# Scale and inverse on one engine, a rounding step taken half a step later, and reordered seams in a four-stage transformer kernel

## The reference

```
x = x + landmark_attention(layernorm(x))    # 16 heads, 32 landmarks, pseudo-inverse, convolution
x = x + ffn(layernorm(x))                   # 128 -> 352 -> 128
x = x + linear_attention(layernorm(x))      # 16 heads of 8, causal running sum
x = x + ffn(layernorm(x))                   # the same weights again
```

```
scale = max(max(|xb|, over 16) / 6, 1e-12)
q     = grid[nearest(|xb / scale|)] * sign(xb) * scale
y     = q(silu(q(x) @ q(Wg).T) * (q(x) @ q(Wu).T)) @ q(Wd).T
```

## Time and profile before

| | |
|---|---|
| median of 3 runs | 839.45 us (836.2 to 840.21) |
| the profiled execution | 839.01 us, span 837.2 us |
| PE busy | 620.6 us, 74% |
| DVE busy | 541.6 us, 65% |
| POOL busy | 317.3 us, 38% |
| ACT busy | 296.0 us, 35% |
| mean granted TensorE clock | 0.899 |

### The profile page before, as it was taken

The page is one execution under the profiler, slowest core; times in us unless marked ns, Lnnn a source line. Parts: engine busy times, 40 slices in busy tenths (PEclk is TensorE's granted clock), DMA queues, the critical chain, the costliest instruction groups (busy, mean ns, idle before and its releaser), DMA issues.

```text
span 837.2 us, 14007 instructions
## 1 busy us (share of the span) xinstructions
PE 620.6 (74%) x5231; PEld 445.8 (53%) x5231; DVE 541.6 (65%) x1078; ACT 296.0 (35%) x523; POOL 317.3 (38%) x408
## 2 busy tenths in 40 slices
PE   2367887888667577598777765899889887777775
PEld 1366784666634334496555554455555554445554
DVE  7624653333188679577888965566667665798874
ACT  2131111333323323314555543333333344555432
POOL 6540000000100000035667888345555544456563
PEclk9996998999988879799898997698999997899997
DMA  8400000000000000000000000000000000000000
GB/s 259 106 1 1 1 0 1 0 1 0 1 2 0 1 1 1 0 2 1 1 1 1 1 1 0 1 2 2 2 2 1 2 2 2 0 16 24 13 25 26
DMA packets 13675, 10.47 MB, mean 13 GB/s; under 512 B 1398, under 2 KB 12598, under 8 KB 13492
## 3 DMA queue, kind: packets, MB, share of 16 engines
q1 hardware_dynamic: 13620, 9.73, 4.2%
HBM read 7.63 MB, written 2.10 MB: 12 GB/s over the span
## 4 chain that ended last, share of the span: by engine, by line
PE 44%; DVE 29%; POOL 11%; issue 9%; ACT 5%; DMA 0%; ACTq 0%; DVEq 0%; POOLq 0%
PE ps L1145 6%; PE ps L1231 5%; PE ps L1362 4%; PE ps L1172 3%; PE ps L1299 3%; PE ps L1381 3%; DVE r L822 3%; DVE ps L904 2%; POOL G L281 2%; PE ps L1260 2%; PE ps L1181 2%; POOL ln L335 2%; DVE S L830 2%; DVE arena L1005 2%; PE ps L1189 2%
## 5 line engine op out<-in xcount | busy, mean ns | idle before, releaser
L335 POOL TENSOR_TENSOR ln<-mv,lnc 128x4 f32<-128x4 f32 x64 | 13.1, 205 | 150.9 <-DVE mv L702 150.9
L354 POOL MEMSET early<- 128x2560 f32 x2 | 4.5, 2232 | 173.3 <-PE ps L1216 163.3
L1231 PE MATMUL ps<-G,xw 128*126 128x512 f32 x72 | 47.6, 814 | 30.2 <-ACT xw L520 22.5
L381 POOL TENSOR_SCALAR_AFFINE_SELECT arena<-arena 128x1024 f32<-128x1024 f32 x32 | 35.0, 1092 | 72.7 <-ACT arena L646 72.7
L1280 PE MATMUL ps<-wguT,xnt 128*128 128x352 f32 x128 | 54.5, 510 | 8.9 <-DVE S L923 8.9
L1299 PEld LDWEIGHTS ps<-wdT,xnt 128*128 128x128 f32 (+1 forms) x384 | 54.2, 216 | 12.5 <-ACT xnt L575 6.4
L1299 PE MATMUL ps<-wdT,xnt 128*128 128x128 f32 (+1 forms) x384 | 55.5, 300 | 2.3 <-ACT xnt L575 2.2
L1278 PE MATMUL ps<-wguT,xnt 128*128 128x352 f32 x128 | 54.0, 506 | 0.5 <-ACT xnt L568 0.2
L1005 DVE TENSOR_TENSOR arena<-ps,tri 128x1024 f32<-128x1024 f32 x32 | 39.2, 1224 | 23.3 <-PE ps L1362 23.3
L646 ACT ACTIVATE arena<-ps 128x1024 f32<-128x1024 f32 x32 | 32.8, 1024 | 49.5 <-PE ps L1362 49.5
L281 POOL TENSOR_TENSOR G<-S,hoff 128x704 f32<-128x704 f32 x32 | 48.6, 1517 | 3.6 <-DVE S L923 1.2
(11 more groups left out here) (197 smaller groups left out, 1570.8 us busy)
## 6 DMA issues: line engine op xcount, KB each, us to landing
X<-in_x SPq DMA_DIRECT2D x8, 256.0 KB, 4.6
out<-X SPq DMA_DIRECT2D x8, 256.0 KB, 2.3
wqkv<-in_wqkv SPq DMA_DIRECT2D x1, 1024.0 KB
band<-in_band SPq DMA_DIRECT2D x1, 897.8 KB
early<-in_wfc SPq DMA_DIRECT2D x1, 512.0 KB
kI<-in_scaled_eye SPq DMA_DIRECT2D x1, 192.0 KB
wattn<-in_wattn SPq DMA_DIRECT2D x1, 192.0 KB, 7.3
S<-in_wd SPq DMA_DIRECT2D x1, 176.0 KB, 3.5
```

The source lines that it names most:

```text
L381: nc.gpsimd.affine_select(out=masked[n % 2][:, 8:16, :], in_=raw.rearrange("p (h t) -> p h t", t=P), pattern=[[0, 8], [1, P]], compare_op= ...
L1231: last = mm(ps[0:WI, w, :], xw[:, w * WO:w * WO + WI], G1[:, b, :], start=True, stop=True)
```

## The change

Six edits, in the order in which they appear below.

- The scale of a block (h and x) is computed by DVE, directly ahead of the reciprocal, and no longer by POOL. The largest magnitudes are written to spare PSUM columns behind the pair (for the first two quads of x to the old place) and read from there.
- DVE's clamp and `move_h` of pair r move from the end of step r to step r+1, between its two `gated`.
- PE takes `down_mms` ahead of the first `gate_up` of a step.
- `lin_norm` is done by ACT, with the bias add left on POOL as `lin_bias`. For quads 0 and 1 it moves to ACT's steps 11 and 15.
- At the seam from the first feed-forward block to the linear attention, POOL's `lin_qk(0)` goes ahead of the residual and the moments of step 16, and PE's product for the denominators goes behind the last step.
- At the seam to the second one, the four steps that are called early are called after tiles 28, 29, 30 and 31 in place of 27, 28, 29 and 31, and ACT normalises the first quad after tile 27.

```diff
-LIN_FILL = {27: -4, 28: -3, 29: -2, 31: -1}
+LIN_FILL = {28: -4, 29: -3, 30: -2, 31: -1}
...
@@ POOL
                 def step(r):
                     q = (r + FILL) // 2
-                    if r % 2 == 0 and q < QN:
-                        need(g, "fx_quant", ffn_quads(p, q))
-                        scales("fx", xblk, ffn_quads(p, q + 1))
-                    if 0 <= r < PN:
-                        need(g, "fh_quant", ffn_pairs(p, r - 1))
-                        scales("fh", hblk[r % 2], ffn_pairs(p, r + 1))
                     if 0 <= r - 1 < PN:
                         quantise_h(r - 1)
                     if r % 2 and q < QN:
                         quantise_x(q)
-                    if p == 0 and 0 <= r - 3 < PN:
+
+                def finish(r):
+                    if 0 <= r - 3 < PN:
                         residual(r - 3)
...
                 step0(r)
-                if r == 12:
-                    lin_norm(0)
+                if r == 16:
+                    lin_qk(0)
+                finish0(r)
...
                 if r == 16:
-                    lin_norm(1)
-                    lin_qk(0)
+                    lin_bias(0)
...
@@ ACT
+            def lin_norm(q):
+                a.wait_ge(s["moment_step"], 2 * TILES + (q + 1) * QD)
+                need(a, "lin_xT_done", q)
+                for k in range(QD):
+                    t = q * QD + k
+                    last = act(xb[:, k, :], X[:, t, :], ACT.Identity, scale=rstd[:, t:t + 1], bias=shift[:, t:t + 1])
+                last.then_inc(s["lin_xb_done"], 1)
...
+                if r == 11:
+                    lin_norm(0)
...
                 if r == 15:
                     lin_exps(0)
+                    lin_norm(1)
...
                 lin_yT(n)
+                if q + 1 < TILES // QD and phase == 3:
+                    lin_norm(q + 1)
...
+                if n == 27:
+                    a.wait_ge(s["lin_qn_done"], QN)
+                    normalise1(0)
...
@@ DVE
-                def inverse(name, b, n):
+                def inverse(name, b, largest, n, free):
+                    v.wait_ge(s[name + "_absmax"], n + 1)
+                    need(v, name + "_quant", free)
+                    ts(out=b[:, 2, :], in0=largest, scalar1=1.0 / 6.0, scalar2=1e-12, op0=ALU.mult,
+                       op1=ALU.max).then_inc(s[name + "_scale"], 1)
                     v.wait_ge(s[name + "_scale"], n + 1)
                     recip(out=b[:, 1, :], in_=b[:, 2, :]).then_inc(s[name + "_inverse"], 1)
+
+                def largest_h(r):
+                    return up_banks(r, F, 2 * F // BLK)[:, 0, :]
...
                         gated(2 * r)
+                    if 0 <= r - 1 < PN:
+                        move_h(r - 1)
+                    if 0 <= r < PN:
                         gated(2 * r + 1)
                         absmax_h(r)
...
-                    if 0 <= r < PN:
-                        move_h(r)
                 return step
...
@@ PE
                 def step(r):
                     q = (r + FILL) // 2
+                    if 0 <= r - 2 < PN:
+                        down_mms(r - 2)
                     if 0 <= r + 1 < PN:
                         gate_up(2 * r + 2)
-                    if 0 <= r - 2 < PN:
-                        down_mms(r - 2)
...
-                if r == 16:
+                if r == 17:
                     lin_den_mms(0)
-                if r == 17:
-                    lin_rdenT(0)
+            lin_rdenT(0)
```

More of the change, by code:

```diff
@@ L261, in ffn @@
             def ffn(p):
-                def scales(name, b, n):
-                    g.wait_ge(s[name + "_absmax"], n)
-                    nc.gpsimd.tensor_scalar(out=b[:, 2, :], in0=b[:, 0, :], scalar1=1.0 / 6.0, scalar2=1e-12, op0=ALU.mult,
-                                            op1=ALU.max).then_inc(s[name + "_scale"], 1)
                 def quantise_x(q):
@@ L303, in step @@
                         quantise_x(q)
-                    if p == 0 and 0 <= r - 3 < PN:
+                def finish(r):
+                    if 0 <= r - 3 < PN:
                         residual(r - 3)
-                    if p == 0 and r >= 6 and r % 2 == 0:
+                    if r >= 6 and r % 2 == 0:
                         layernorm_moments(2, (r - 6) // 2)
-                return step
+                return step, finish
             g.memset(wn, 0.0).then_inc(s["wn_zeroed"], 1)
@@ L354, in _, with lin_bias @@
                 g.memset(vbd[k], 0.0).then_inc(s["vbd_zeroed"], 1)
-            step0, step1 = ffn(0), ffn(1)
-            def lin_norm(q):
-                g.wait_ge(s["moment_step"], 2 * TILES + (q + 1) * QD)
-                need(g, "lin_xT_done", q)
-                for k in range(QD):
-                    t = q * QD + k
-                    last = nc.gpsimd.tensor_scalar(out=xb[:, k, :], in0=X[:, t, :], scalar1=rstd[:, t:t + 1],
-                                                   scalar2=shift[:, t:t + 1], op0=ALU.mult, op1=ALU.add)
-                last.then_inc(s["lin_xb_done"], 1)
+            (step0, finish0), (step1, _) = ffn(0), ffn(1)
+            def lin_bias(q):
                 g.wait_ge(s["lin_xb_done"], q + 1)
@@ L414, in _ @@
                     if phase == 3 and q + 1 < TILES // QD:
-                        lin_norm(q + 1)
+                        lin_bias(q + 1)
                 if n % QD == 1 and n > QD:
@@ L653, in _ @@
             a.wait_ge(s["b_loaded"], 16 * 6)
+            normalise0(0)
             for r in ATT_FILL.values():
@@ L876, in absmax_x @@
                     v.wait_ge(s["fx_norm"], n + 1)
-                    reduce(out=xblk[:, 0, :].unsqueeze(1), in_=blocks(x_blocks()), axis=AX, op=ALU.max,
+                    reduce(out=largest_x(q).unsqueeze(1), in_=blocks(x_blocks()), axis=AX, op=ALU.max,
                            apply_absolute_value=True).then_inc(s["fx_absmax"], 1)
@@ L907, in absmax_h @@
                     v.wait_ge(s["f_h"], ffn_tiles(p, 2 * r + 2))
-                    reduce(out=pair(hblk[r % 2][:, 0, :]), in_=blocks(up_banks(r)), axis=AX, op=ALU.max,
+                    reduce(out=pair(largest_h(r)), in_=blocks(up_banks(r)), axis=AX, op=ALU.max,
                            apply_absolute_value=True).then_inc(s["fh_absmax"], 1)
```

22 lines of the change are left out of this document (12 added, 10 removed).

## The result

The changed kernel takes 814.62 us (median of 4, 812.91 to 816.35); the kernel before, timed beside it, 839.83 (836.2 to 841.73). The ratio is 0.9714, 95% interval 0.9683 to 0.9746: 2.9% faster. The profiled execution took 816.01 us for a span of 814.3, where 818.5 was forecast for it.

What follows compares the result with a forecast made beforehand. DVE was taken as fullest in both feed-forward blocks, PE in the linear attention. Terms of -1, -10.5, -1.5, 0, -3 and -4.5 sum to -20.5 from 839.0: 818.5 profiled, 819 us on the median, range 810 to 832.

Steps and rivals of the forecast that it cites:

- the clamp that still pays for POOL: Rival, chance 0.13: DVE's clamp still meets POOL's work at each step's start; 828 us, up to 832.
- the scale that waits for POOL: Rival, chance 0.04: DVE's scale waits until `quantise_x` on POOL has read the old one; 830 us.
- DVE alone setting the step: Rival, chance 0.10: down product in time, even step of the second block 6.8 us; 812 and below to 808.
- PE's clock: Rival, chance 0.05: PE falls to 1.2 GHz in 13 middle pairs of steps, 2.5 us each; 847 us.
- The layout by start-to-start times: Count of feed-forward steps by engine: second block 7.5 us even, 6.1 odd; first block 13.3 a pair.
- First block, -10.5: First feed-forward block: shorter steps and a vanished 3.14 us wait give -12, less 1.5 set aside for PE's clock.
- Second block, -4.5: Second feed-forward block: a gain of 6 us from shorter steps, less 1.5 set aside for PE's clock.
- My own mark for a wrong prediction: Second block's even steps over 8 us, from the clock or an ACT chain longer than 3.2, would refute the prediction.
- First seam, -1.5: Seam to the linear attention: 5.5 us of POOL work leave the path, part given back; between -4 and +1.
- `lin_norm`, 0: Linear attention: moving `lin_norm` from POOL to ACT changes nothing, between -1.5 and +1 us.
- Second seam, -3: Seam to the second block: DVE's 4.6 us of waits go, scales cost 0.4; between -4.5 and -1.
- Attention output, -1: Attention output: two waits of 0.78 us become 0.2 each, -1 us.

Runs made afterwards that it cites:

- E4: The changed kernel with ACT's normalisation of the next quad behind `hT_copy` of the even step, not at the end of the odd one: 807.45 us.
- E12: E4 with gate/up first in the first feed-forward block and the down product first in the second: 801.37 us.
- E7: The changed kernel with only the seam from the first feed-forward block to the linear attention ordered as before: 818.25 us.
- E8: The changed kernel with the four early steps of the second block behind tiles 27, 28, 29 and 31, as before: 808.01 us.
- E6: E3 and E4 together, on the changed kernel: 804.85 us.
- E3: The changed kernel with PE's old order, gate and up ahead of the down product: 807.74 us.
- E1: The changed kernel with DVE's clamp and sum put back to the end of their own step, scale still on DVE: 844.31 us.
- E9: The changed kernel with `lin_norm` back on POOL ahead of `lin_bias`, at the places of before: 817.98 us.
- E10: The kernel before with only DVE's clamp and sum of h half a step later, scales on POOL: 824.23 us.
- E11: The kernel before with only the scale on DVE, from largest values in PSUM: 839.43 us.
- E2: The changed kernel with the scales back on POOL ahead of `quantise_h`, largest values in on-chip memory again: 821.55 us.
- E5: E1 and E3 together: the changed kernel with the sum in its own step and gate/up first: 835.32 us.

## Why the prediction was right

**The time.** The forecast of 819 stood 4.4 us, 0.5%, above the 814.62; the mechanism was the forecast's. That it stood so close is in part luck: the terms were off by 0.8 to 3.4 us, in both directions, and most of that cancelled. Of the rivals, the clamp that still pays for POOL fell with its median of 345 ns, the scale that waits for POOL with the 48 reciprocals, and DVE alone setting the step with the waits at the residual, 7.0 us in the second block. PE's clock did fall in the middle of the blocks, but at a price near 6 us, not 32. That price was also summed wrongly: it counts 13 middle pairs of steps where the layout has five and six, and eleven pairs at 2.5 us give 843 in place of 847.

**The steps.** The layout by start-to-start times was right to 0.1 us for both steps of the second block where PE ran at its full clock, and in the first block the pairs from step 6 on, 13.5, 13.4 and 13.4, answer to the 13.3 given; the two pairs ahead of them took 14.9 and 14.6, and only the first of these met a lower clock. E4 and E12 show the reason given, ACT's normalisations in the chain ahead of the down product.

**First block, -10.5 against -13.9.** The term is -12 less 1.5 set aside for the clock. Nothing had to be set aside: the granted clock of this block rose from 0.91 to 0.97 in the profiled execution. E7 and E8 leave the block as it is in the changed kernel and took 101.0 both at 0.95, so the gain is 11.5 there, with less help from the clock.

**Second block, -4.5 against -1.8 with the end.** Here the allowance of 1.5 was too small. E8 shows the block at a clock of 0.97: 98.5, a gain of 8.1 where I counted 6. The surplus lies in the steps without x work: steps 12 to 14 went from 20.8 us to 16.7, 1.4 a step where I gave 0.6. At 0.92 the block takes 104.4: the clock costs 5.9. My own mark for a wrong prediction, even steps over 8 us, was met by three steps, for the first of the two reasons named with it.

**TensorE's order.** "The edit that puts it ahead of `gate_up` saves it the time of one `gate_up` here" was half of the account. It saves it only where DVE waits for the product and nothing else holds it up: in the second block with the normalisations out of the chain (E12's 92.7 against E6's 97.6, both at 0.98), and hardly with them in it (E8's 98.5 against E3's 99.1). In the first, where the residual is not on DVE, `gate_up` and with it the SiLU and the next offset stand behind it, 3.3 us (E3), of which 2.2 show as DVE's waits for the offset (4.4 to 2.2). That `gate_up` itself would be late was not priced.

**First seam, -1.5 against -3.9.** Half of what is given back was priced too dear: the denominators follow the down product at 508.74 without a wait, and that product took 1.60 us, not twice 1.5. The 2 us for `move_h(15)` were right: E1, with the sum in its own step, has 22.0 us here against 23.9. E7 gives the order 4.0, with the clock's part in it, and E9 says that it also needs `lin_norm` off POOL, 3.1 of it: the two don't add.

**`lin_norm`, 0.** Right for the linear attention (157.4 in E9 against 156.8), wrong to speak of that alone: it holds the first seam.

**Second seam, -3 against -3.8.** How much of it the scale earned is not settled. The 24.5 us of before stand at a clock of 0.79; E10, whose edit doesn't touch this seam, has 21.7 at 0.92, still with 3.3 us of waiting for the scale, and E11 has 18.3 at 1.00 with none. That makes 3.4 at most for the old fill. With the late fill it is 0.4: E2 has 21.1 and the changed kernel 20.7, both at 0.84. The late fill costs 0.4 at like clock (E8).

**Attention output, -1 against +2.** The two waits are gone; the stretch from 300 us on ran at a clock of 0.85, against 0.89 before. In E8 the same code took 87.29 us from 300 on at 0.90, 2.9 less than before, the next two rows being the changed kernel and E8:

```profile
300.00:392.18 92.18, 72.90 (x873) 56.76 (x874) 70.52 (x178) 25.58 (x40) 13.44 (x31) 0.85 0.00 1
```

```profile
300.00:387.29 87.29, 67.70 (x871) 52.52 (x870) 67.89 (x173) 24.74 (x38) 13.44 (x31) 0.90 0.00 1
```

Whether the edit is worth its 1 us here can't be told from this: E10, which leaves the stage as it was before, came to the first block at 389.03, 1.2 sooner than before.

**What I had not seen** is how the two main edits hang together. I laid out the steps with both in place, and never asked what each would do alone. Alone they bring -12.8 (E10) and +2.4 (E11), -10.4 together. Both in one kernel, with gate/up first (E3, 807.7) and less the 4.0 us of the first seam (E7), stand at some 812, an estimate, which is 26 below the 837.9 timed beside E3. The half step by itself is worth 12.8 with the scale on POOL (E10) and 27.6 with it on DVE (E5 against E3). Steps 0 to 15 of the two blocks together, and in them DVE's clamps and two of its waits, in us:

| kernel | two blocks | all clamps | waits for POOL's scale | waits for ACT's offset |
|---|---|---|---|---|
| before | 219.0 | 24.2 | 13.0 | 12.9 |
| E11 scale on DVE | 226.3 | 31.7 | 0 | 18.0 |
| E10 half step | 202.4 | 16.9 | 12.7 | 5.1 |
| E5 scale on DVE, sum in own step | 229.2 | 31.2 | 0 | 19.5 |
| E3 scale on DVE, half step | 194.4 | 16.9 | 0 | 5.3 |

The scale on DVE lets POOL run into a clamp and has DVE reach the next clamp before the offset is there; the half step takes both away. It moves the sum, POOL's start behind it and the clamps, so that the clamp of the tokens' offset costs 466 ns and not 1204. From E5 to E3 the clamps give 14.3 of the 34.8 us and the offset's waits 14.2; from before to E10 they give 7.4 and 7.8 of 16.7. How much of the rest is the clock (0.86 and 0.88 in E5, 0.98 in E3) wasn't taken apart.

**Open.** Why PE's clock stayed up in the second block of E3, E4, E6, E8, E10 and E12 (0.97 to 0.98) and fell in that of the changed kernel, E7 and E9 (0.92). The length of the steps doesn't tell: in the changed kernel step 6 took 7.58 us at the full clock, and step 8 took 7.58 at 0.81. Every execution of E8 (807.47 to 808.87) is below every one of the changed kernel (812.91 to 816.35), so it is no matter of one run, but no run here tells what decides.

## What to carry to other kernels

Price edits together where one engine's wait keeps another engine out of a conflict: an instruction that looks like waste on POOL (a scale of 0.36 us that waits) may be what holds its long ones off a clamp on DVE. Try each edit alone and both together: here one alone was worth nothing and doubled what the other was worth. Lay out an even and an odd step by start-to-start times, engine by engine; it gave the steps to 0.1 us, and it names the next edit (what stands ahead of the late product in its engine's queue), which here brought another 1.6%, together with the first block's old order. Look for the granted clock of each stretch before a gain or loss of a few us is given to a cause, and set a stretch beside one of another run with the same instructions: half of E4's gain and all of E3's in the second block were the clock.

## What the hardware showed

- A short DVE instruction with its source in PSUM doesn't pay for POOL. The scale of h from PSUM took 193 to 204 ns in all 32 cases, of which 24 started while a POOL instruction ran; the one at 747.72 took 0.19 in the midst of one. The same kind of operation with its source in on-chip memory took 182 ns at the median of four and 974 once, started 0.16 us after a mask of POOL and done 0.04 after it. POOL at both places, then DVE at 683.50:

```profile
683.34 1.09 POOL L365 TENSOR_SCALAR_AFFINE_SELECT arena<-arena 128x1024 f32<-128x1024 f32 x1
...
746.67 1.39 POOL L279 TENSOR_TENSOR band<-G,hblk 128x704 f32<-128x704 f32 x1
```

```profile
683.50 0.97 DVE L868 TENSOR_SCALAR xblk<-xblk 128x32 f32<-128x32 f32 x1
```

  (The page "GPSIMD Engine Reference" of the Trainium skill, section Key points, says that GpSimd shares its interfaces to on-chip memory with VectorE and contends with its instructions in a 2-port mode. The trace agrees with that, 974 against 182.)
- A bf16 clamp that starts while a long instruction of POOL runs ends 0.15 (128x512) or 0.2 us (128x704) after it, in E11 as in the earlier trace rows, so it costs up to the whole of that: 1.50 us for one of 0.26. Who comes first decides: the clamps of 1.50 us started 0.03 after POOL's instruction, and in the kernel before the clamp at 783.88, 0.03 ahead of one, took 0.34.
- The clock is worth as much as an edit: one and the same block took 98.5 us at a granted clock of 0.97 (E8) and 104.4 at 0.92 (the changed kernel), with DVE busy for 85.97 us in both.
